# A value convolution on TensorE and thirteen extra wide products in a layer loop

## The reference

```python
def _short_conv(x, w):                 # w: [256, 4], one filter of 4 taps per channel
    xp = jnp.pad(x, ((0, 0), (K - 1, 0), (0, 0)))
    y = jnp.zeros_like(x)
    for k in range(K):
        y = y + xp[:, k:k + L, :] * w[:, k]
    return y

q, k, v = (silu(_short_conv(x @ W.T, c)) for W, c in ((Wq, conv_q), (Wk, conv_k), (Wv, conv_v)))
beta = sigmoid(x @ Wb.T)
q, k = _l2norm(q), _l2norm(k)          # per head of 16 channels
o, S = _delta_rule(q, k, v, beta)      # v_new = (v - k S) * beta; S += k v_new; o = q S
out = rms_norm_per_head(o) * o_norm_w @ Wo.T
```

## Time and profile before

| | |
|---|---|
| median of 3 runs | 3272.19 us (3272.04 to 3273.61) |
| the profiled execution | 3270.95 us |
| its span, first to last instruction | 3269.1 us |
| mean granted TensorE clock | 0.862 |
| PE, PEld, DVE, ACT, POOL busy | 80%, 59%, 65%, 49%, 34% |

### The profile page before, as it was taken

How to read it: one execution, slowest core, us unless ns; L and a number is a source line. 1 busy time by engine, 2 the same in 40 slices (tenths; PEclk the granted TensorE clock), 3 DMA queues, 4 the chain that set the end, 5 groups by cost and what they waited for, 6 DMA issues and landing times. The chain is left out here.

```text
span 3269.1 us, 110359 instructions
## 1 busy us (share of the span) xinstructions
PE 2601.0 (80%) x45968; PEld 1940.2 (59%) x45968; DVE 2126.1 (65%) x5160; ACT 1595.1 (49%) x2896; POOL 1107.2 (34%) x1092
## 2 busy tenths in 40 slices
PE   4578888888888887886787888888987898897666
PEld 2355555556555555654566666667776666675443
DVE  4878998888899888886352111122323577677996
ACT  5455555555555554551143333344444666656442
POOL 0000343333333332334235555555554333233000
PEclk8778898888888888886698989989999899999877
DMA  2000122222112221222256777677779676673521
GB/s 68 8 10 4 63 75 70 70 70 68 61 64 77 70 72 61 70 103 79 70 182 214 223 224 225 218 228 231 238 223 359 219 272 220 235 259 139 221 100 26
DMA packets 191587, 448.68 MB, mean 137 GB/s; under 512 B 34034, under 2 KB 83700, under 8 KB 182772
## 3 DMA queue, kind: packets, MB, share of 16 engines
q1 hardware_dynamic: 129652, 284.26, 27.6%
q0 software_dynamic: 52224, 148.97, 12.0%
q10 hardware_dynamic: 9216, 8.39, 0.8%
HBM read 266.07 MB, written 175.42 MB: 135 GB/s over the span
## 5 line engine op out<-in xcount | busy, mean ns | idle before, releaser
L1041 POOL DMA_INDIRECT scr_xs<-xn_r,idx x512 | 534.5, 1044 | 1183.5 <-PE ps L473 458.3
L1067 POOL DMA_INDIRECT scr_ys<-y,idx_t x576 | 572.5, 994 | 733.9 <-issue 496.4
L712 PE MATMUL ps<-xT,wr 128*128 128x256 f32 (+1 forms) x2560 | 600.0, 380 | 123.1 <-issue 117.2
L2060 DVE TENSOR_TENSOR h<-sg,ps 128x256 f32<-128x256 f32 x320 | 125.2, 393 | 714.8 <-ACT sg L1337 434.7
L712 PEld LDWEIGHTS ps<-xT,wr 128*128 128x128 f32 x2560 | 458.8, 201 | 192.3 <-issue 142.5
L720 PE MATMUL ps<-wr,h 128*128 128x256 f32 x1152 | 324.8, 402 | 63.2 <-ACT y L1345 61.7
L1345 ACT ACTIVATE y<-ps,of_row 128x256 f32<-128x256 f32 x576 | 245.8, 476 | 179.9 <-remote 78.3
L1337 ACT ACTIVATE sg<-ps 128x256 f32<-128x256 f32 x320 | 117.0, 366 | 383.0 <-remote 186.8
L720 PEld LDWEIGHTS ps<-wr,h 128*128 128x128 f32 x1152 | 226.9, 203 | 102.7 <-issue 71.7
L527 PE MATMUL ps<-sq,w_proj 128*128 128x512 f32 x512 | 259.1, 644 | 5.0 <-issue 2.3
L1685 DVE TENSOR_TENSOR tu<-tu,tmp 128x60 f32<-128x60 f32 (+14 forms) x480 | 242.5, 505 | 16.5
(11 more groups left out here) (268 smaller groups left out, 4256.0 us busy)
## 6 DMA issues: line engine op xcount, KB each, us to landing
wr<-in_wexp SPq DMA_DIRECT2D x224, 384.0 KB
xt<-scr_xs SPq DMA_DIRECT2D x256, 280.0 KB
yg<-scr_ys SPq DMA_DIRECT2D x64, 1024.0 KB
scr_ys<-y,idx_t POOLq DMA_INDIRECT x576
scr_xs<-zeros SPq DMA_DIRECT2D x64, 140.0 KB
xt<-scr_xs SPq DMA_DIRECT2D x64, 140.0 KB
x_in<-in_x SPq DMA_DIRECT2D x64, 128.0 KB
x_res<-in_x SPq DMA_DIRECT2D x64, 128.0 KB, 2.7
```

Source lines behind the costliest of these rows:

```text
L712: last = pe.matmul(ps[:, bank, half * TILE:half * TILE + wide], wr[:, w % NW, at:at + EI], xT2[:, t % NH, k, 0:wide], start=k == 0, stop=k ...
L1041: nc.gpsimd.indirect_dma_start(xs[int(i >= FIRST)][:, :], bass.IndirectOffsetOnAxis(idx[:, i % NR, c, k:k + 1], 0), xn_r[:, i % NR, c, :], ...
L1067: nc.gpsimd.indirect_dma_start(ys[int(t >= NTH[0])][:, :], bass.IndirectOffsetOnAxis(idx_t[:, t % NRT, r:r + 1], 0), y2[:, t % NY, r, :], ...
```

## The change

Three things are edited.

1. The value's four taps become matrix products. A new constant `v_taps` holds, for each value group g and tap k, the identity times the column of tap k: a diagonal 128x128 matrix (eight of them, made on DVE at the start). `value_taps(i, g)` on PE multiplies four shifted views of `raw` by them and sums in a ring bank. ACT's `value_silus(i, g)` reads that bank, applies the silu and writes `conv`. DVE's `taps(a, 4, 5)` and ACT's scaled copy for n = 4, 5 are gone, and `silus` now serves n < 4 with s_conv and s_silu counted by four an iteration; `new_inputs` waits for the new semaphore s_values.
2. `busy_ahead(n)` and `busy_behind(n)` multiply n times the identity by 256 columns of `w_proj` into columns that nothing reads from (bank RU, which the next step overwrites, and the unused half of bank QP). They stand once inside each `solved` and each `to_output` (eight an iteration), three ahead of `from_state(j, 0)`, and two ahead of `to_output(j, 3)`.
3. `w_quant` and `bias_row` take addresses that the first phase's buffers leave free, so `bias_row` is loaded among the later constants.

```diff
@@ PE
+            def busy_ahead(n):
+                for _ in range(n):
+                    pe.matmul(ps[:, RU, 0:D], identity[:], w_proj[:, 0, 0, :], start=True, stop=True)
+            def busy_behind(n):
+                for _ in range(n):
+                    pe.matmul(ps[:, QP, D:2 * D], identity[:], w_proj[:, 0, 0, :], start=False, stop=True,
+                              skip_group_check=True)
...
 def solved(j, c):                      # the same in to_output(j, c)
+                    if u == H // 2:
+                        busy_ahead(1)
...
+            def value_taps(i, g):
+                n = 2 * G + g
+                bank = into(f"TAP{n}", i)
+                ring.emptied(pe, f"PROJ{n}", i)
+                for k in range(KC):
+                    last = pe.matmul(ps[:, bank, :].rearrange("p (b t) -> p b t", b=B), v_taps[:, g, k, :],
+                                     raw[:, n, :, k:k + TB], start=k == 0, stop=k == KC - 1)
+                done(last, bank)
...
                 if C:
+                    if j:
+                        busy_ahead(3)
                     from_state(j, 0)
...
                 if C:
                     to_output(j, 1)
                 if A:
+                    value_taps(a, 1)
                     project(a, 7)
                     project(a, 4)
...
                     to_output(j, 2)
                 if A:
+                    value_taps(a, 0)
                     norms(a, 0)
...
                 if C:
+                    busy_behind(2)
                     to_output(j, 3)
                     to_state(j, 3)
@@ ACT
-                    nc.scalar.activation(conv[:, n, :]..., by_chunk, ACT.Copy, scale=conv_w[...])
+                    if n < 2 * G:
+                        nc.scalar.activation(conv[:, n, :]..., by_chunk, ACT.Copy, scale=conv_w[...])
...
+            def value_silus(i, g):
+                n = 2 * G + g
+                bank = ring.filled(act, f"TAP{n}", i)
+                if i:
+                    act.wait_ge(s_bv, i)
+                last = nc.scalar.activation(conv[:, n, :], ps[:, bank, :], ACT.Silu)
+                last.then_inc(s_xe[bank], 1)
+                ring.emptied(act, f"TAP{n}", i)
+                act.sem_inc(s_values, 1)
...
                     gate(p, 0)
                 if A:
+                    value_silus(a, 1)
                     betas(a, 1)
...
                     silus(a, 3)
+                    value_silus(a, 0)
                     raised(a, 0)
                     raised(a, 1)
-                    silus(a, 4)
...
                     norm_roots(a)
-                    silus(a, 5)
@@ DVE
+            for g in range(G):
+                for k in range(KC):
+                    sI.did(V.tensor_scalar(v_taps[:, g, k, :], identity[:], conv_w[:, 2, g, k:k + 1], None, ALU.mult))
...
             def new_inputs(i):
-                dve.wait_ge(s_silu, 6 * (i + 1))
+                dve.wait_ge(s_values, 2 * (i + 1))
...
-                if A:
-                    taps(a, 4, 5)
                 if C:
                     new_state(j, 2)
```

More of the change, by code:

```diff
@@ L168, in network_kernel @@
         identity = sb("identity", [P, P])
-        w_quant = sb("w_quant", [P, G, D])
         one_col = sb("one_col", [P, 1])
@@ L207, in network_kernel @@
         zeros = sb("zeros", [P, 2 * ROW])
-        bias_row = sb("bias_row", [1, 2 * D])
         ones_mean = sb("ones_mean", [P, 2 * NS])
@@ L214, in network_kernel @@
         w_proj = sb1("w_proj", [P, G, 4, D])
+        v_taps = sb1("v_taps", [P, G, KC, P])
         ones_head = sb1("ones_head", [P, P])
@@ L310, in network_kernel @@
         quantT = sb("quantT", [P, G, N])
+        w_quant = sb("w_quant", [P, G, D])
+        bias_row = sb("bias_row", [1, 2 * D])
         qa0, qb0, qc0 = xq[:].rearrange("p c d -> p (c d)")[:, 0:G * D], qb[:, 0:G * D], qc[:, 0:G * D]
@@ L338, in network_kernel @@
         s_silu = sem("s_silu")
+        s_values = sem("s_values")
         s_sq = sem("s_sq")
@@ L394, in network_kernel @@
                      (w_o[:], wo), (w_gate[:], wgate), (gbias_row[:], gbrow), (lower_tri[:], lower),
-                     (w_shared[:], wshared), (bias_row[:, 0:D], brow[0:1, :]),
-                     (bias_row[:, D:2 * D], brow[0:1, :]),
+                     (w_shared[:], wshared),
                      (ones_mean[:], mean), (b_delta[:], bdelta))
@@ L400, in network_kernel @@
                            for b in range(B))
+        later += tuple((bias_row[:, m * D:(m + 1) * D], brow[0:1, :]) for m in range(2))
         ALL_CONST = 16 * len(constants)
@@ L1101, in _ @@
         def _(act):
-            CONV_ORDER = (2, 3, 0, 1, 4, 5)
+            CONV_ORDER = (2, 3, 0, 1)
             def root(ph, i):
@@ L1176, in raws @@
                     by_chunk = ps[:, bank, :].rearrange("p (c b t) -> p b c t", c=NC, b=B)
-                    nc.scalar.activation(conv[:, n, :].rearrange("p (b c t) -> p b c t", b=B, c=NC), by_chunk,
-                                         ACT.Copy, scale=conv_w[:, n // G, n % G, HIST:])
+                    if n < 2 * G:
+                        nc.scalar.activation(conv[:, n, :].rearrange("p (b c t) -> p b c t", b=B, c=NC), by_chunk,
+                                             ACT.Copy, scale=conv_w[:, n // G, n % G, HIST:])
                     nc.scalar.activation(raw[:, n, :, HIST:].rearrange("p b (c t) -> p b c t", c=NC), by_chunk,
@@ L1191, in silus @@
                 for n in ns:
-                    act.wait_ge(s_conv, 6 * i + CONV_ORDER.index(n) + 1)
+                    act.wait_ge(s_conv, 4 * i + CONV_ORDER.index(n) + 1)
                     nc.scalar.activation(conv[:, n, :], conv[:, n, :], ACT.Silu).then_inc(s_silu, 1)
-                    if n < 2 * G:
-                        act.wait_ge(s_silu, 6 * i + n + 1)
-                        nc.scalar.activation(sq[:, n, :], conv[:, n, :], ACT.Square).then_inc(s_sq, 1)
+                    act.wait_ge(s_silu, 4 * i + n + 1)
+                    nc.scalar.activation(sq[:, n, :], conv[:, n, :], ACT.Square).then_inc(s_sq, 1)
+            def value_silus(i, g):
[7 more added lines that the diff above has]
+                act.sem_inc(s_values, 1)
             def raised(i, *ns):
@@ L1629, in key_rows @@
             def key_rows(i):
-                dve.wait_ge(s_silu, 6 * i + 4)
+                dve.wait_ge(s_silu, 4 * (i + 1))
                 V.tensor_tensor(conv[:, G:2 * G, :], conv[:, G:2 * G, :], sq[:, G:2 * G, :], ALU.mult)\
```

## The result

The changed kernel takes 3367.31 us (median of four runs, 3358.48 to 3377.88) against 3272.9 for the kernel before, run beside it: ratio 1.0289, interval 1.0258 to 1.0321. It is slower by 2.9%; forecast were 3234 us and a range that ended at 3320. The profiled execution took 3377.88 us, the longest of the four, with a span of 3376.1.

The account below looks back on a forecast made before the run. Neither PE nor DVE alone bounds the loop: PE its first stage, DVE its second, nearly tied in the third. Fourteen iterations at -2.5 (-35), last two -6, start +3: -38 us, forecast 3234, range 3205 to 3262.

Parts of the forecast that it names:

- DVE's lost taps: 0: In the third part of each iteration, six taps removed from DVE gain 0, with 4.06 us as the bound.
- The taps on PE, 7.5 us: Eight added 512-column products cost PE 7.5 us an iteration, 3.76 in each of its second and third parts.
- Thirteen wide products at 0.47 each, 6.1 in all: Thirteen added 256-column products an iteration cost PE 0.47 us each, 6.1 in all; bounds 0 and 0.8 each.
- The clock gives 8.2 us back, held at 0.95: PE's existing products get 8.2 us an iteration back if the clock is held throughout; taken as mostly held, about 0.95.
- Stage I gains 2.5 us: The iteration's first part, 27.5 us, where DVE waits for the pair products, gets 2.5 us shorter.
- PE enters stage III 1.0 late: PE adds 5.2 us in the iteration's second part, has 4.3 idle there, and enters the third about 1.0 us late.
- Waits covered, 7.7: In the forecast's totals, 7.7 us of PE's waits an iteration are covered, against 13.6 us of added work.
- Stage III: 0: The iteration's third part, 32.1 us, with the value taps and the norms, keeps its length: 0 us.
- Start +3: At the start, eight 128x128 products on DVE and the second tap group ahead of the first norms add 3 us.
- The last two iterations -6: The loop's last two iterations get 3 us shorter each, -6 together, with bounds of +12 and -16.
- The rival that came true: PE becomes the bound in the iteration's second and third parts, clock not following: +3.3 us an iteration, 3320 us; chance 0.30.

Follow-up runs that it names:

- the outer ones: Kernel before plus only five 256-column products, two ahead of to_output(j, 3) and three ahead of from_state(j, 0): ratio 1.0000.
- half the columns: Kernel before with pair products of 32 columns instead of 64 from the second block on: ratio 0.9993.
- the taps alone: Changed kernel without its thirteen 256-column products, the value's taps staying on TensorE: ratio 1.0116, and 1.0119 when run once more.
- the inner ones alone: Kernel before plus only the eight 256-column products in the middle of solved and to_output: ratio 1.0148.
- the runs with 16 columns: Thirteen products 16 columns wide instead of 256: in the changed kernel ratio 1.0289, added to the kernel before 1.0116.
- the taps with the outer ones: Changed kernel without its eight 256-column products inside solved and to_output: ratio 1.0020 in one job, 1.0087 in another.

## Why the prediction was wrong, step by step

- *DVE's lost taps: 0.* Right (1.0001). The 4 us went in stage III: DVE works 24.5 us there instead of 28.3 and waits more.
- *The taps on PE, 7.5 us.* Right in size: 70.0 / 9 = 7.8. By themselves 1.2%, some 2.8 us an iteration over fourteen.
- *Thirteen wide products at 0.47 each, 6.1 in all.* Wrong, the first failed step. The price was read from products that stand in a row of their kind. Between tile products it is 0.74 to 0.76, and 0.43 to 0.46 is left with 16 columns. Busy time of the two groups is (76.3 + 14.5) / 9 = 10.1 us an iteration. The sum by stages also placed eleven of the thirteen: those inside the last solved and the last to_output were in none of its terms, and the five behind the norms were put down at 0.2 as filling waits, which holds where they stand alone (1.0000). Nine stand in stage III and take 6.8 us there by start-to-start times.
- *The clock gives 8.2 us back, held at 0.95.* Wrong in size. It is 0.92 on average, but 0.85 in stage III (0.79 in the iteration shown), where it was hoped to be over 0.9. The pair products give 1.7 us (98.9 to 83.6 over nine; 3.0 forecast), the norms 1.6 (1.7 forecast), the shared expert 0.4 (2.2 forecast), the projections nothing (1.3 forecast). From the busy times, 7.8 + 10.1 - 12.3 = 5.6 in all.
- *Stage I gains 2.5 us.* Wrong: 0.3, though the products shrank. The issue waits ahead of them rose from 16.5 to 20.6 us, and PE's wait for pt from 6.1 to 11.6. The runs with the outer ones and with half the columns showed the same without the taps: shorter pair products are worth nothing to the kernel's time here.
- *PE enters stage III 1.0 late.* It was about 3: 5.5 us were added in stage II (3.5 of taps, 2.0 of wide ones), and its idle time, 4.2, fell to 1.8, so it gave up 2.4. The forecast took all of its 4.3.
- *Waits covered, 7.7.* 5.0.
- *Stage III: 0.* It was +7.3, which is the whole loss of an iteration. 3.9 of taps, 6.8 of wide ones and 3.0 of lateness, less 1.6 and 1.3 for norms and from_state, and less 3.7 of idle time (7.5 to 3.8), make 7.1; the rest is spread over smaller groups.
- *Start +3.* Right: the first r_sb moved from 135.55 to 138.11. *The last two iterations -6.* From their start to the last r_sb it is 164.6 before and 175.8 after, +11, near the far bound of +12. The wide ones were paid there: the same stretch takes 161.1 us in the run with the taps alone and 177.3 with the inner ones alone.

In totals, the sum of the forecast and the measured iteration lie 9.6 us apart. 4.3 of it is added work (17.9 us, not 13.6), 2.6 the clock's return (5.6, not 8.2) and 2.7 the waits covered (5.0, not 7.7).

The rival that came true is the one that called PE the bound, at the place it named, stage III. Its condition (the return and the covered waits fall below what is added) was met with 5.6 and 5.0; but the added work was 17.9 us, not 13.6, so its 3320 was too low as well. Its name, that the clock does not follow, is wrong: the clock followed, and by the runs with 16 columns it paid about for the columns that raised it, not for the rest.

By the rule on the share of LDWEIGHTS (Trainium skill, Perfetto Trace Analysis, Identifying the Most-Contended Engine) PE would still have had room: the share is 538.58 of 909.21 us, 59%, while DVE waits 7.2 us for it. The trace disagrees with the rule here, as far as this share goes; MFU, the measure that the section names beside it, was not worked out.

## What to carry to other kernels

Price a matrix product by its neighbours: between products of another tile size it also takes the gaps on both sides, and a row of its own kind doesn't show that. Before work is moved off an engine, take it away without putting it elsewhere: here one run, with a ratio of 1.0001, shows that there was nothing to win by relieving DVE. And a higher TensorE clock need not shorten the kernel: with the outer ones it shortened the pair products by 13.6 us over nine iterations and the kernel by nothing.

## What the runs showed of the hardware

- A 128x128 product between 32x32 ones takes 0.43 to 0.46 us from tile start to tile start with 16 columns and 0.74 to 0.76 with 256 (both instructions of a float32 product, full clock).
- Sixteenfold columns at the same places cost nothing in the end that these runs can tell. With the taps, 16 columns gave 1.0289 and 256 columns 1.0272 and 1.0289; without the taps, 1.0116 and 1.0134. The granted clock of the nine iterations was 0.85 against 0.92, and 0.84 against 0.90.
- Jobs differ in more than a factor: the kernel before took 3048 us in one and 3249 in another, and the taps with the outer ones stood at 1.0020 and 1.0087 beside it. The cause is open.
